# Attention of a gated cross-attention block: next keys and values projected inside the attention steps, keys laid out in small blocks, split weights kept in DRAM

## The reference

```
q = layernorm(x) @ Wq            # 32 query heads of 32
k, v = ctx @ Wk, ctx @ Wv        # 8 key/value heads, each for 4 query heads
a = softmax(q k^T / sqrt(32)) v  # per batch entry, 128 x 128
x = x + tanh(g_xattn) * (a @ Wo)
n = layernorm(x)
x = x + tanh(g_ffn) * ((silu(n @ W_gate^T) * (n @ W_up^T)) @ W_down^T)   # F = 2752
```

## Time and profile before

| | |
|---|---|
| median of 3 runs | 2156.32 us |
| the profiled execution | 2159.85 us |
| its span (first to last instruction) | 2158.1 us |
| TensorE busy (matmul) | 2040.7 us, 95% |
| VectorE busy | 1313.8 us, 61% |
| ScalarE busy | 917.6 us, 43% |
| POOL busy | 628.4 us, 29% |
| mean granted TensorE clock | 0.979 |

### The profile page before, as it was taken

How to read it: one execution, slowest core, us unless ns; L and a number is a source line. 1 busy time by engine, 2 the same in 40 slices (tenths; PEclk the granted TensorE clock), 3 DMA queues, 4 the chain that set the end, 5 groups by cost and what they waited for, 6 DMA issues and landing times.

```text
span 2158.1 us, 30150 instructions
## 1 busy us (share of the span) xinstructions
PE 2040.7 (95%) x9800; PEld 1704.7 (79%) x9800; DVE 1313.8 (61%) x2234; ACT 917.6 (43%) x2218; POOL 628.4 (29%) x473
## 2 busy tenths in 40 slices
PE   7989799988989989999999899999999999999999
PEld 5878688777878868888888687877888888778877
DVE  6886787779678876455454265566455454434555
ACT  4782476267337634333333244444333333233334
POOL 1340232123113344444444120112444444300000
PEclk9999899999999999999999999999999999999999
DMA  5105313310430322222122457574222122236666
GB/s 185 50 31 197 107 40 125 140 69 30 176 108 30 137 103 83 87 87 87 67 79 78 141 177 250 171 272 163 88 87 83 67 82 87 99 126 204 213 225 220
DMA packets 79084, 261.94 MB, mean 121 GB/s; under 512 B 8832, under 2 KB 25728, under 8 KB 73600
## 3 DMA queue, kind: packets, MB, share of 16 engines
q1 hardware_dynamic: 78976, 260.61, 34.5%
HBM read 221.25 MB, written 39.32 MB: 121 GB/s over the span
## 4 chain that ended last, share of the span: by engine, by line
PE 75%; DVE 12%; ACT 5%; issue 4%; DMA 3%; POOL 0%; SPq 0%; POOLq 0%; DVEq 0%; ACTq 0%
PE ps L1421 24%; PE ps L1423 24%; PE ps L1422 24%; DVE kb_h L1041 3%; ACT pb L728 2%; DVE nmx L1056 1%; DMA dr<-in_wd 1%; DVE kb_l L1043 1%; PE ps L1461 1%; DVE pt_l L994 1%; DMA x<-in_x 1%; DVE qo_l L994 1%; PE ps L1452 1%; DVE qo_l L1030 1%; DVE dl L994 1%
## 5 line engine op out<-in xcount | busy, mean ns | idle before, releaser
L1421 PE MATMUL ps<-xop_h,w_h 128*128 128x512 f32 x1208 | 474.4, 393 | 6.9 <-ACT x1c L671 5.0
L1423 PE MATMUL ps<-xop_h,w_l 128*128 128x512 f32 x1208 | 472.4, 391 | 0.0
L1422 PE MATMUL ps<-xop_l,w_h 128*128 128x512 f32 x1208 | 472.4, 391 | 0.0
L1421 PE MATMUL ps<-dh,hh 128*128 128x512 f32 x672 | 267.0, 397 | 14.2 <-DVE dl L994 9.0
L1421 PEld LDWEIGHTS ps<-xop_h,w_h 128*128 128x128 f32 x1208 | 228.0, 189 | 54.8 <-ACT x1c L671 5.9
L1423 PEld LDWEIGHTS ps<-xop_h,w_l 128*128 128x128 f32 x1208 | 228.3, 189 | 47.9
L1422 PEld LDWEIGHTS ps<-xop_l,w_h 128*128 128x128 f32 x1208 | 228.2, 189 | 46.7
L1423 PE MATMUL ps<-dh,hl 128*128 128x512 f32 x672 | 263.4, 392 | 0.0
L1422 PE MATMUL ps<-dl,hh 128*128 128x512 f32 x672 | 263.4, 392 | 0.0
L994 DVE TENSOR_TENSOR w_l<-fraw,w_h 128x512 fp32r<-128x512 f32 x130 | 129.3, 995 | 208.5 <-ACT w_h L671 208.5
L570 POOL TENSOR_TENSOR pb<-pb,rinv 128x512 f32<-128x512 f32 x128 | 152.7, 1193 | 324.6 <-DVE rinv L1061 324.6
(11 more groups left out here) (159 smaller groups left out, 3959.6 us busy)
## 6 DMA issues: line engine op xcount, KB each, us to landing
dr<-in_wd SPq DMA_DIRECT2D x132, 512.0 KB, 4.1
fraw<-in_wf SPq DMA_DIRECT2D x42, 1024.0 KB, 5.3
wc_raw<-in_wc SPq DMA_DIRECT2D x44, 512.0 KB, 4.0
hd<-hb SPq DMA_DIRECT2D x42, 512.0 KB, 2.9
hr<-hd SPq DMA_DIRECT2D x84, 192.0 KB, 3.1
wr_raw<-in_wr SPq DMA_DIRECT2D x24, 512.0 KB, 3.3
x<-in_x SPq DMA_DIRECT2D x5, 2048.0 KB, 8.4
x1d<-x SPq DMA_DIRECT2D x16, 512.0 KB, 2.6
```

The source lines that it names most:

```text
L1421: pe.matmul(out, w_hi_, m_h, start=first, stop=False, skip_group_check=goes_on)
L1422: pe.matmul(out, w_hi_, m_l, start=False, stop=False, skip_group_check=goes_on)
L1423: return pe.matmul(out, w_lo_, m_h, start=False, stop=last, skip_group_check=goes_on)
```

## The change

- **Keys and values of the next group in the steps.** `kv_part` projects one k-slice of an entry; two slices (three in the last two) run in each of steps 19 to 33 of groups 0 to 2, in banks 6 and 7. `kt`, the copies `kv_out` and `kt_out`, and the splits of the context (steps 17, 19, 24, 28) move into the steps too. Keys and values stay in float32 in two sets (`kc[g % 2]`, `vc[g % 2]`), without a remainder of their own.
- **q slices.** Three a step in groups 0 to 2 (up to step 14), two a step in group 3. All q tiles use banks 6 and 7, so tile i >= 2 waits for the remainder of tile i-2.
- **Key blocks.** `build_kb(g, a, b, j)` makes one small block: two rounding copies into `kb_h`, a wait for them, and a subtraction into `kb_l`. Half 1 is made in steps 10 to 19, one or two small blocks a step; half 0 of the next group after the steps. `build_vp` likewise rounds, waits and subtracts. POOL clears the layouts once.
- **Weights.** In group 0 each split tile is also written to DRAM (`wcs`, `wrs`, high and low part, 512 KB each); groups 1 to 3 load both parts straight into the slots. A Wo tile of e >= 4 is loaded when its slot is free (`o_first`). Columns 0 and 1 of the next group load when the projection is through.
- **Between groups.** The parts of entry 3 leave the steps (groups 0 to 2). After the steps come e = 0 to 3 for entries 1, 3, 2, then e = 4 to 7 in the order 3, 0, 1, 2, with the eight half transposes of the next x (`xt1`) among them, in banks 6 and 7.
- The loop over groups is written out on every engine.

```diff
-COL_STEP = {5: 0, 6: 5, 7: 9, 8: 32, 9: 33}
-ROW_STEP = {0: 1, 1: 13, 2: 17, 3: 21}
-KB_STEPS = (12, 13, 17, 20)
+Q_PRE = 4
+KV_BEGIN = 19
+KV_SLICES = (2,) * 13 + (3, 3)
+COL_STEP = {5: 0, 6: 3, 7: 5, 8: 8, 9: 11, 10: 13, 11: 16}
+ROW_STEP = {0: 1, 1: 6, 2: 10, 3: 14}
+CT_STEP = (17, 19, 24, 28)
+KB_STEPS = {}
+for _b in range(NB):
+    for _j in range(4):
+        KB_STEPS.setdefault(10 + 2 * _b + _j, []).append((_b, _j))
...
 def q_bank(i):
-    return 4 * i if i < 2 else 6 + i % 2
+    return 6 + i % 2
...
+            def load_row(g, e):
+                if g == 1 and e < RS:
+                    sp.wait_ge(r_kept[e], 64)
+                if e < RS:
+                    sp.wait_ge(o_done, g * NB)
+                else:
+                    sp.wait_ge(o_first, g * RS + (e - RS + 1))
+                sp.dma_start(wr_h[:, e % RS, :].bitcast(F32), wrs[e, 0]).then_inc(r_in[e % RS], 16)
+                sp.dma_start(wr_l[:, e % RS, :].bitcast(F32), wrs[e, 1]).then_inc(r_in[e % RS], 16)
...
+            def boundary(g):
...
+                load_xn(g + 1, 0)
+                load_xn(g + 1, 1)
+                load_xn(g + 1, 2)
+                load_xn(g + 1, 3)
+                load_column(g + 1, 0)
+                load_column(g + 1, 1)
+                if g == 0:
+                    load_wr(7)
+                load_x1(g)
+                if g > 0:
+                    for e in range(RS, NO):
+                        load_row(g, e)
+                load_column(g + 1, 2)
...
-            def build_kb(g, a, b):
-
-                for j in range(4):
-                    for half in range(2):
-                        rows = slice(half * H2 + j % 2 * HD, half * H2 + j % 2 * HD + HD)
-                        src = slice(j * HD, (j + 1) * HD)
-                        keys, cols = slice(b * P, (b + 1) * P), slice(j * P, (j + 1) * P)
-                        nc.vector.tensor_copy(kb_h[rows, b, cols], kc_h[src, a, keys].bitcast(F32))
-                        if rows == src:
-                            ins = nc.vector.tensor_copy(kb_l[rows, b, cols], kc_l[src, a, keys].bitcast(F32))
-                ins.then_inc(kb_built, 1)
+            def build_kb(g, a, b, j):
+
+                keys, cols = slice(b * P, (b + 1) * P), slice(j * P, (j + 1) * P)
+                src = slice(j * HD, (j + 1) * HD)
+                for half in range(2):
+                    rows = slice(half * H2 + j % 2 * HD, half * H2 + j % 2 * HD + HD)
+                    ins = nc.vector.tensor_copy(kb_h[rows, b, cols], kc[g % 2][src, a, keys])
+                ins.then_inc(kb_rounded, 1)
+                dve.wait_ge(kb_rounded, len(KB_ORDER) * g + KB_ORDER.index((a, b, j)) + 1)
+                ins = minus(kb_l[src, b, cols], kc[g % 2][src, a, keys], kb_h[src, b, cols])
+                if j == 3:
+                    ins.then_inc(kb_built, 1)
...
             def body(g, last):
-                dve.wait_ge(kb_zero, g + 1)
-                dve.wait_ge(k_lo, g * NB + NB)
-                dve.wait_ge(v_lo, g * NB + NB)
-                for b in range(NB):
-                    build_kb(g, 0, b)
+                if g == 0:
+                    dve.wait_ge(kb_zero, 1)
+                    dve.wait_ge(k_ready, NB)
+                    for b in range(NB):
+                        for j in range(4):
+                            build_kb(0, 0, b, j)
                 build_vp(g, 0)
                 build_vp(g, 1)
-                split_wc(g, 4)
+                if g == 0:
+                    split_wc(4)
                 q_out(g, 0)
                 q_out(g, 1)
...
+                    if g == 0:
+                        split_wr(4)
                     stats1_next(G, 0)
                     stats1_next(G, 1)
-                    normalise1(G, 0, xn[:, 0, :])
-                    normalise1(G, 1, xn[:, 1, :])
+                    if g == 0:
+                        split_wr(5)
+                    dve.wait_ge(s_done, g * UNITS + UNITS)
+                    dve.wait_ge(k_ready, G * NB + NB)
+                    for b in range(NB):
+                        for j in range(4):
+                            build_kb(G, 0, b, j)
+                        if b == 0:
+                            normalise1(G, 0, xn[0][:, :])
+                            normalise1(G, 1, xn[1][:, :])
+                            stats1_next(G, 2)
+                            stats1_next(G, 3)
+                            if g == 0:
+                                split_wr(6)
+                        if b == 2:
+                            normalise1(G, 2, xn[2][:, :])
+                            normalise1(G, 3, xn[3][:, :])
+                            if g == 0:
+                                split_wr(7)
...
             def q_tile(g, i, ks):
                 if ks[0] == 0:
-                    pe.wait_ge(wc_lo, wcn(g, i) + 1)
-                    if i >= 4:
+                    if g == 0:
+                        pe.wait_ge(wc_lo, wcn(i) + 1)
+                    else:
+                        pe.wait_ge(c_in[i % CS], columns_in(g, i))
+                    if i >= 2:
                         pe.wait_ge(q_lo, g * NQ + (i - 1))
...
+            def kv_part(G, b, k):
...
+                ins = three(ps[:, 6 + b % 2, :].rearrange("p (s m) -> p s m", s=CS),
+                            ct_h[:, b % 2, k, :], ct_l[:, b % 2, k, :], wc_h[:, :, k, :], wc_l[:, :, k, :],
+                            k == 0, k == K8 - 1)
+                if k == K8 - 1:
+                    ins.then_inc(kv_done, 1)
...
+                if g > 0:
+                    pe.wait_ge(x1_add, g * YN)
                 for n in range(STEPS):
-                    if n < UNITS - 10:
-                        q_part(n + 2)
+                    for _ in range(queries[n] if n < len(queries) else 0):
+                        i, k = next(q_slice)
+                        q_tile(g, i, (k,))
+                    if not last and 0 <= n - KV_BEGIN < len(KV_SLICES):
+                        for _ in range(KV_SLICES[n - KV_BEGIN]):
+                            kv_part(g + 1, *next(kv_slice))
...
```

More of the change, by code:

```diff
@@ L640, in _ @@
                 rsqrt1(0, t, t + 1)
-            with pool.Fori(0, NG - 1) as g:
+            clear()
+            for g in range(NG - 1):
                 body(g, False)
@@ L1734, in _ @@
             kt(0, 3)
-            with pe.Fori(0, NG - 1) as g:
-                body(g, False)
-            body(NG - 1, True)
+            for g in range(NG):
+                body(g, g == NG - 1)
             for s in range(NS):
```

690 lines of the change are left out of this document (390 added, 300 removed).

## The result

The changed kernel takes 2188.72 us (median of four runs, 2186.39 to 2192.06) against 2155.23 for the kernel before (2152.14 to 2157.72): ratio 1.0148, 95% interval 1.0122 to 1.0173. It is slower, as forecast, by 33.5 us where 21 were forecast, and inside the likeliest case's own range. Here and in the experiments, single executions that took far longer (3402 us in E4, 9062 in E4b, the profiled 4110 in E6) are left out of the ratios. The profiled execution is the one of 2186.39 us, span 2184.6.

The account below looks back on a forecast made before the run. TensorE, busy for 95% of the span, was taken as the bound, with VectorE setting the pace where key blocks are built. Stage terms summed to 813.0 us of attention against 792.0, giving 2178 against 2156.32; range 2140 to 2207.

Parts of the forecast that it names:

- the likeliest case's own range: Whole kernel: the main forecast of a slower kernel with its surroundings, 2163 to 2195 us, chance 0.47.
- gap before q tile 2 of group 0: Before group 0's steps: TensorE stands 11 us while VectorE makes key blocks ahead of the q remainder.
- stall for the rows' DMA: Boundaries of groups 1 and 2: Wo rows 4 to 7 queue behind x and columns; 4 us, 4.5 after group 3.
- the row of 413: Fullest slice of the DMA view, 413 GB/s, used to price 10 MB at the boundaries at 25.4 us.
- the steps of groups 0 to 2: Attention steps with the projection moved in: 134 us in group 0, 128 in groups 1 and 2.
- the work (111.3): TensorE's work in the steps: 94.8 plus 22.7 of projection, minus 5.5 of output matmuls and 0.7 of a slice.
- 13 of stall beside the blocks: Steps 11 to 19 of groups 1 and 2: TensorE stalls some 13 us for VectorE, with blocks at 0.9 us.
- the 38.0 of VectorE: VectorE's summed work in steps 11 to 19, 38.0 us against 24 of TensorE, including 1.2 for the context split.
- 2 for the banks: Steps of groups 0 to 2: q tiles sharing banks 6 and 7 wait for earlier remainders, about 2 us.
- Rival C: Whole kernel: no change, blocks near 0.7 us and stalls of 9, 2157 us; chance 0.14.
- Rival A: Whole kernel: faster, small blocks at 0.6 us, stall 7 in place of 13, 2143 us; chance 0.24.
- Rival B: Whole kernel: slower still, blocks at 1.2 us because copies meet POOL's normalisation, 2203 us; chance 0.15.

Follow-up runs that it names:

- E4: Changed kernel with q slices at 3 a step for 10 steps, then 2, and the projection from step 20: 2182.23 us, ratio 1.0127 to the kernel before.
- E4b: Changed kernel with q slices at 2 a step for ten steps, then 4, projection unaltered: 2182.08 us, ratio 1.0120 to the kernel before.
- E6: Changed kernel with the next keys' transposes and their copies one step later: 2201.11 us, ratio 1.0219 to the kernel before; no usable profile.
- E7: Changed kernel with only entry 0's key blocks before the first q remainder in group 0, the others behind: 2183.03 us, ratio 1.0139 to the kernel before.
- E8: Changed kernel with Wo row splits and normalisation before the key blocks of entries 1 to 3 at the boundaries: 2200.24 us, ratio 1.0202 to the kernel before.
- E1: Changed kernel with q tiles 0 and 1 back in banks 0 and 4, so tile 2 waits for nothing: 2185.03 us, ratio 1.0144 to the kernel before.
- E3: Changed kernel without the 16 key blocks of half 1 in steps 10 to 19: 2152.05 us, ratio 0.9982 to the kernel before.
- E2: Changed kernel with each key block's low part a plain copy, without wait and subtraction: 2183.04 us, ratio 1.0124 to the kernel before.
- C2: Changed kernel with banks 0 and 4, x by entry, and first blocks and row splits reordered, slices as in the changed kernel: 2179.26 us, ratio 1.0112.
- E9: Changed kernel computing only two of eight k-slices of each entry's key and value projection: 2182.4 us, ratio 1.0117 to the kernel before.
- C1: Changed kernel with banks 0 and 4, x by entry, first blocks and row splits reordered, plus redistributed q and projection slices: 2167.27 us, ratio 1.0053.

## Why the prediction was right, and where its sizes were off

**Direction and places held.** By its own steps, forecast and measured: gap before q tile 2 of group 0 11 and 9.7; start of group 0 28 and 28.3; boundary of group 0 56 and 55.5, with 11.5 and 9.6 (7.9 and a shorter one) for Wo's remainders; start of groups 1 and 2 15.7 and 15.6; boundaries 48.7 and 46.9; stall for the rows' DMA 4 and 3.1 in the boundary of group 1, beside 0.9 for transposed x, and 4.5 and 4.4 at the end of group 3; group 3 15, 107, 45.8 and 15.0, 105.4, 45.0. E7, E8 and E1 show for the gaps of group 0 that they were the order of VectorE's list and the shared bank: with the cause taken away, the first went in E7 and shrank from 9.7 to 4.9 in E1, the second from 9.6 to 1.9 in E8. The transfers that the prediction counted in the boundary of group 1 (window):

```profile
407.80:433.00 25.20, 23.65 (x115) 19.54 (x114) 18.21 (x57) 1.04 (x3) 3.33 (x8) 1.00 1.02 401
```

They moved 401 GB/s over 25.2 us, where the prediction had 25.4 us by the row of 413. The Trainium skill ("DMA: Bandwidth & Descriptors", "Where 436 GB/s comes from") has about 358 GB/s as the limit of HBM traffic of one core. The trace doesn't agree: this stretch, all of it DRAM traffic of one core, is 12% above it, and the stall came out near the 4 of the row and not at the 7 of that figure.

**The term that was mis-sized is the steps of groups 0 to 2**: 139.1, 133.8 and 135.3 against 134, 128 and 128, 18.2 us too much, of which the other stages gave 7.8 back (attention ended 10.4 late). In group 1 the work (111.3) can't be far off: E3, at a clock of 0.99, is busy for 112.9. The idle time was 16.7 against 15. The clock was the larger miss: 2 forecast, 117.14 - 111.3 = 5.8 measured, at 0.95; in group 0 it was 118.99 - 111 = 8 for the same 2.

**The reason given for the stall was half right, and its total came near by luck.** Term by term in group 1: 13 of stall beside the blocks, and 9.2 measured, with the context's split that the 38.0 of VectorE contain; 2 for the banks, and 4.4 measured in the three waits before q tiles; nothing for the copy `kn` before the key transposes, and 3.0 measured. A stall too large by 4 covered two terms too small by 5. A block took 0.78 instead of 0.9. Rival C had stalls of 9 beside the blocks, which is what came, and called the whole a tie; what it lacked is the other waits and the clock. E3 shows that blocks as such cost 8 to 11 us a group in the changed kernel; E2 shows that 0.16 less a block is returned by the clock in groups 0 and 1. Rival A (faster, decided below 0.65 a block) is thereby wrong in its mechanism too: with blocks of 0.62 the kernel is still 1.2% slower than before.

What the change adds in the steps beyond its work is 10 to 12 us a group, by the control group 3 and by E3. The trace of the changed kernel divides it, group 1 against group 3: 7.5 more of idle time (16.7 against 9.2), which are the 4.4 before q tiles and the 3.0 for `kn`, and 4.4 of half-clock time (117.14 - 96.19 of busy time for 16.5 of work).

Rival B (blocks at 1.2 through POOL) named a mechanism that is there. Every one of the 41 roundings of a value block that met a normalisation on POOL took 0.72 to 0.99 us and ended 0.08 after it; the 23 that met none took 0.22. One of each kind (timelines of VectorE and POOL):

```profile
305.04 1.04 POOL L719 TENSOR_TENSOR pb<-pb,rinv 128x512 f32<-128x512 f32 x1 [3.37 <-DVE rinv L1209]
305.18 0.98 DVE L1198 CAST vp_h<-vc 128x128 fp32r<-128x128 f32 x1
...
319.90 1.04 POOL L719 TENSOR_TENSOR pb<-pb,rinv 128x512 f32<-128x512 f32 x1 [3.37 <-DVE rinv L1209]
321.61 0.22 DVE L1198 CAST vp_h<-vc 128x128 fp32r<-128x128 f32 x1
```

That is 7.9 us of VectorE in the steps of group 1, where the kernel before lost 5.6. The roundings of key blocks met it seldom, 4 of 32 in these steps for 0.7 us in all, and none of the new subtractions did. So B's size was wrong for key blocks, and its cause is at work in the kernel before too.

**What it comes down to.** Groups 1 and 2 break even, since the 25 to 30 us that start and boundary give are taken by steps that grew by 27 to 29 for 16.5 of work. Group 0 gains nothing from kept weights, still makes every split, and pays the new steps: its start and its steps grew by 9.8 and 33.6, its boundary gave 9.4 back, and that is the 34 us. C2, with the slices as they were, takes 15.8 + 145.6 + 45.5 = 206.9 there instead of 222.9: 16 of them are the orders and banks, though its S1 is 3.0 longer and attention as a whole ends 14.1 earlier.

**Open:** why E6 is slower by 12 us (a usable profile of it would tell); how much of the 10 to 12 us a group would come back if one of its waits were removed, since less idle time or less work came back as half-clock time in E2 and E9; what the writing of kept weights costs group 0, which no run leaves out; and whether the projection between groups, with the rest of the change kept, would be faster, which no run tried.

## What to carry to other kernels

- Work moved under a pipeline is hidden only if the pipeline's own chain has room: E9 left out three quarters of the moved projection and won 6 us in the median. Ask of each moved piece which copy must leave PSUM for it, and what stands ahead of that copy in its engine's list.
- Order a list by who asks first: the four blocks that the first scores need, then the remainder that TensorE waits for, then the rest (E7, C1). The same move made at another place (E8) put the rest in front of the next remainder and lost.
- A group of the same kernel that lacks one part of the change is a free control; read it before building experiments, and list first what else differs in it.
- A wait in a table of totals is worth placing in time: two of the three before q tiles stand ahead of the first key block, and an experiment on the first bank (E1) can't move them.
